# Moving the second gram and the row of norms by one tile in a fused graph attention with a residual layer norm

## What is computed

```python
z_l = x @ W_lang.T ;  z_g = x @ W_grav.T ;  v = x @ W_V.T            # per batch of x
zn  = z_l / max(norm(z_l), EPS)
A_l = max(zn @ zn.T, 0) * not_eye
d2  = max(sq + sq.T - 2 * z_g @ z_g.T, 0)                            # sq = row sums of z_g * z_g
A_g = exp(-d2 / (2 * sigma**2)) * not_eye
K   = w_l * row_stochastic(A_l * adj) + (1 - w_l) * row_stochastic(A_g * adj)
out = layernorm(x + (K @ v) @ W_O.T)                                 # over the last axis
```

## Time and profile before

| | us |
|---|---|
| median of 3 runs | 969.12 (967.76 to 969.14) |
| the profiled execution | 971.3 |
| span of the profile | 969.6 |
| busy: TensorE / VectorE / ScalarE / GpSimd | 956.4 / 699.6 / 323.6 / 146.3 |

### The profile page before, as it was taken

The page is one execution under the profiler, slowest core; times in us unless marked ns, Lnnn a source line. Parts: engine busy times, 40 slices in busy tenths (PEclk is TensorE's granted clock), DMA queues, the critical chain, the costliest instruction groups (busy, mean ns, idle before and its releaser), DMA issues.

```text
span 969.6 us, 13226 instructions
## 1 busy us (share of the span) xinstructions
PE 956.4 (99%) x4802; PEld 827.4 (85%) x4802; DVE 699.6 (72%) x1954; ACT 323.6 (33%) x632; POOL 146.3 (15%) x155
## 2 busy tenths in 40 slices
PE   9999999999999999999999999999999999999997
PEld 7888888988888888888888889888888988889885
DVE  4567768767785777858677786777858767685588
ACT  5333243232422423243232432423233232432331
POOL 2002120021200212110021200212101121200231
PEclk9999999999999999999999999999999999999999
DMA  8322353442534434353442534434344442533001
GB/s 218 86 61 80 100 144 101 114 154 86 120 109 114 147 101 119 108 141 99 120 143 81 136 105 119 146 98 122 107 114 126 120 131 93 136 98 120 1 23 66
DMA packets 215872, 106.78 MB, mean 110 GB/s; under 512 B 140544, under 2 KB 187648, under 8 KB 215808
## 3 DMA queue, kind: packets, MB, share of 16 engines
q1 hardware_dynamic: 189504, 92.04, 34.1%
q10 hardware_dynamic: 26304, 13.90, 4.9%
HBM read 63.44 MB, written 42.47 MB: 109 GB/s over the span
## 4 chain that ended last, share of the span: by engine, by line
PE 90%; DVE 5%; DMA 3%; issue 1%; ACT 0%; POOL 0%; ACTq 0%; POOLq 0%; SPq 0%; DVEq 0%
PE ring L333 22%; PE ring L334 22%; PE ring L335 22%; PE g_bank L333 8%; PE g_bank L335 8%; PE g_bank L334 8%; DMA off<-off_turned 1%; DMA off_turned<-off 1%; DMA k_turned<-ag 1%; PE g_bank L328 1%; DVE al L928 1%; DVE al L905 0%; DVE bn L966 0%; DVE kT_lo L761 0%; DMA y<-in_x_dram 0%
## 5 line engine op out<-in xcount | busy, mean ns | idle before, releaser
L747 DVE TENSOR_TENSOR zg_lo<-ring,zg_hi 128x512 fp32r<-128x512 f32 x64 | 43.9, 690 | 103.3 <-ACT zg_hi L575 103.2
L1180 POOL TENSOR_TENSOR rstd<-var_eps,neg_half 128x1 f32<-128x1 f32 x64 | 41.5, 650 | 416.7 <-DVE var_eps L974 416.7
L333 PE MATMUL ring<-xT_hi,wgT_hi 128*128 128x512 f32 x256 | 102.0, 398 | 0.0
L333 PE MATMUL ring<-xT_hi,wlT_hi 128*128 128x512 f32 x256 | 101.1, 395 | 0.0
L334 PE MATMUL ring<-xT_lo,wgT_hi 128*128 128x512 f32 x256 | 100.1, 391 | 0.0
L335 PE MATMUL ring<-xT_hi,wgT_lo 128*128 128x512 f32 x256 | 99.8, 390 | 0.0
L334 PE MATMUL ring<-xT_lo,wlT_hi 128*128 128x512 f32 x256 | 99.7, 390 | 0.0
L335 PE MATMUL ring<-xT_hi,wlT_lo 128*128 128x512 f32 x256 | 99.7, 390 | 0.0
L333 PE MATMUL ring<-wvo_hi,xT_hi 128*128 128x512 f32 x256 | 99.7, 389 | 0.0
L335 PE MATMUL ring<-wvo_hi,xT_lo 128*128 128x512 f32 x256 | 99.6, 389 | 0.0
L334 PE MATMUL ring<-wvo_lo,xT_hi 128*128 128x512 f32 x256 | 99.6, 389 | 0.0
(11 more groups left out here) (126 smaller groups left out, 2211.9 us busy)
## 6 DMA issues: line engine op xcount, KB each, us to landing
xb<-in_x_dram SPq DMA_DIRECT2D x60, 256.0 KB, 4.6
out_dram<-y SPq DMA_DIRECT2D x60, 256.0 KB, 2.0
k_turned<-ag SPq DMA_DIRECT2D x56, 256.0 KB, 2.5
y<-in_x_dram SPq DMA_DIRECT2D x14, 1024.0 KB, 7.1
off_turned<-off SPq DMA_DIRECT2D x28, 384.0 KB, 2.3
al<-k_turned SPq DMA_DIRECT2D x112, 64.0 KB, 2.3
al<-k_turned ACTq DMA_DIRECT2D x112, 64.0 KB, 2.6
off<-off_turned SPq DMA_DIRECT2D x56, 96.0 KB, 2.4
```

Of the source, the lines that this page charges most:

```text
L333: nc.tensor.matmul(psum, lh, rh, start=k == 0, stop=False)
L747: nc.vector.tensor_tensor(pair[1][:, i, :], bank[:, :], pair[0][:, i, :].bitcast(F32), ALU.subtract).then_inc(evacuated, 1)
L1180: nc.gpsimd.tensor_tensor(rstd[:, i:i + 1], var_eps[:, i:i + 1], neg_half[:, 0:1], ALU.pow)\
```

## The change

In each of the batches 0 to 13 TensorE's `gram_l` moves behind zg tile 3 (it was ahead of it), and the row of norms moves behind zl tile 0 (it was ahead of it). The ring order `BATCH` swaps these two tiles; `LAST`, which had them so already, keeps its order. ScalarE reads zg tile 3 out ahead of `widen_r` instead of behind it, zl tile 0 ahead of the fetch of the off blocks, and zl tile 1 ahead of the mirror copies. VectorE's splits move likewise: zg tile 3 ahead of the diagonals, zl tiles 0 and 1 ahead of `mask_al`; the four steps of `mask_ag` are mixed with the diagonals in another way. SyncE's and GpSimd's orders stay as they are; no instruction is added or removed.

```diff
--- before.py
+++ after.py
@@ -60,11 +60,11 @@
 
 
 
-BATCH = ([("zg", 1, 0), ("hsq", 0, 0), ("zg", 1, 1), ("zg", 1, 2), ("zg", 1, 3), ("r", 0, 0), ("zl", 1, 0),
+BATCH = ([("zg", 1, 0), ("hsq", 0, 0), ("zg", 1, 1), ("zg", 1, 2), ("zg", 1, 3), ("zl", 1, 0), ("r", 0, 0),
           ("zl", 1, 1), ("zl", 1, 2), ("zl", 1, 3), ("u", 1, 0), ("u", 1, 1), ("u", 1, 2), ("u", 1, 3)]
          + [("out", 0, i) for i in range(4)])
 
-LAST = (BATCH[:5] + [BATCH[6], BATCH[5]] + BATCH[7:10]
+LAST = (BATCH[:10]
         + [("u", 1, 0), ("kT", 0, 0), ("kT", 0, 1), ("out", 0, 0), ("hsq", 1, 0), ("kT", 0, 2), ("kT", 0, 3),
            ("out", 0, 1), ("out", 0, 2), ("r", 1, 0), ("u", 1, 1), ("u", 1, 2), ("u", 1, 3), ("kT", 1, 0),
            ("out", 0, 3), ("kT", 1, 1), ("out", 1, 0), ("kT", 1, 2), ("out", 1, 1), ("kT", 1, 3), ("out", 1, 2),
@@ -504,10 +504,11 @@
                 s.hsq_as_rows(0)
                 s.project("zg", 1)
                 s.project("zg", 2)
+                s.project("zg", 3)
                 s.gram_l(0)
-                s.project("zg", 3)
+                s.project("zl", 0)
                 s.r_as_rows(0)
-                for i in range(T):
+                for i in range(1, T):
                     s.project("zl", i)
                 for i in range(T):
                     s.project("u", i)
@@ -674,14 +675,15 @@
                 s.exp(0, 1)
                 s.exp(0, 2)
                 s.exp(0, 3)
+                s.hi("zg", 1, 3, zg)
                 s.widen_r(0)
                 s.scale_ag(0, range(1))
-                s.hi("zg", 1, 3, zg)
+                s.hi("zl", 1, 0, zl)
                 fetch_off(act, "l", s.b, ACT_PARTS)
                 s.scale_ag(0, range(1, T))
-                s.hi("zl", 1, 0, zl)
+                s.hi("zl", 1, 1, zl)
                 s.copy_mirrors("l", gl_copied, range(T))
-                for i in range(1, T):
+                for i in range(2, T):
                     s.hi("zl", 1, i, zl)
                 s.hi("u", 1, 0, u[1 - parity])
                 fetch_k(act, b, 0, ACT_PARTS)
@@ -989,21 +991,21 @@
                     s.exponent(0, i, copied=True)
                 s.mask_ag(0, 0)
                 s.lo("zg", 1, 2, zg)
+                s.mask_ag(0, 1)
+                s.lo("zg", 1, 3, zg)
+                s.mask_ag(0, 2)
                 s.diagonals(0, gl_rows, 1.0, nsq, gl_diag, [0], turned=gl_off)
-                s.mask_ag(0, 1)
-                s.mask_ag(0, 2)
+                s.mask_ag(0, 3)
                 s.diagonals(0, gl_rows, 1.0, nsq, gl_diag, [1], turned=gl_off)
-                s.mask_ag(0, 3)
+                s.scale_of_ag(0)
                 s.diagonals(0, gl_rows, 1.0, nsq, gl_diag, [2], turned=gl_off)
-                s.scale_of_ag(0)
                 s.diagonals(0, gl_rows, 1.0, nsq, gl_diag, [3], turned=gl_off)
                 s.clamp_norms(0)
-                s.lo("zg", 1, 3, zg)
+                s.lo("zl", 1, 0, zl)
                 s.repeat_row("r", 0)
-                s.lo("zl", 1, 0, zl)
+                s.lo("zl", 1, 1, zl)
                 s.mask_al(0, 0, copied=True)
                 s.mask_al(0, 1)
-                s.lo("zl", 1, 1, zl)
                 s.mask_al(0, 2)
                 s.mask_al(0, 3)
                 s.scale_of_al(0)
```

## The result

| | before | after |
|---|---|---|
| median of 11 runs, us | 967.83 (967.37 to 969.60) | 976.54 (972.24 to 977.98) |
| profiled execution, us | 971.3 | 977.83 |
| span of the profile, us | 969.6 | 976.1 |

The ratio of the changed kernel to the one before is 1.0076, 95% interval 1.0062 to 1.0091: slower by 0.76%, some 7.4 us; the two medians of the table lie 8.7 us apart. 975.7 was forecast, from 970.0 to 980.5.

The account below looks back on a forecast made before the run. The prediction took TensorE, busy 956.4 of 969.6 us, to bound the kernel. Its terms, -4.16 + 7.7 + 3.1 = +6.6 us, added to a median of 969.12, gave 975.7 us, range 970.0 to 980.5.

Parts of the forecast that it names:

- The gain: Second gram's waits for VectorE's exponent in batches 4, 7 and 11 all go: -4.16 us.
- The margin: Exponent's spare time before the second gram, to grow from 0.6 to 3.3 us.
- The row of norms, cost 0: On TensorE, r_wide and the r transpose move alike, one tile still between gram and r transpose: cost 0.
- The shift of 2.66 us, fixed by GpSimd's fourth tile: Fourth mask_al on VectorE starts 2.66 us later, held by GpSimd's fourth mask_r tile until 849.76 in batch 13.
- It goes through whole to kT tile 0: From the fourth mask_al through turn_k, k store, ScalarE's fetch and kT_hi to kT_lo, the 2.66 us passes undiminished.
- First aggregate tile, 7.7 us: TensorE waits for kT tile 0 before the first aggregate tile: 0.24 us in batch 13, 7.7 us over 14 batches.
- Second aggregate tile, 3.1 us: TensorE waits for kT tile 1 before the second aggregate tile: 0.37 us in batch 13, 3.1 us over 14 batches.
- VectorE late into the next batch, cost 0: VectorE enters the next batch some 1.7 us late, putting 0.4 us on the off transfer, within 3.3 us: cost 0.
- The sum: Whole kernel: -4.16 + 7.7 + 3.1 = +6.6 us, giving 975.7 us.
- The clock: Rival: after long waits in batches 3 and 10, aggregate tiles run at 1.2 GHz: +5.4, 981 us, chance 0.03.
- the signs of being wrong: First kT_lo under 2.4 us later, VectorE idle before mask_al not for GpSimd, TensorE waits elsewhere, granted clock below 1.00.
- The faster rival: mask_r's fourth tile does not hold mask_al, or k stores land sooner: shift 1.66, -2.1 us, 967.0 us, chance 0.09.

Follow-up runs that it names:

- its control: Kernel before, with mask_r's tile 0 made by VectorE instead of GpSimd: 968.43 us, ratio 0.9994.
- VectorE's tile: Kernel after, with mask_r's tile 0 made by VectorE, so that GpSimd makes three tiles: 967.28 us, ratio 0.9982 to the kernel before.
- four extra tiles: Kernel before, with four extra GpSimd tiles of mask x row ahead of its four, in batches 0 to 13: 1016.74 us, a single run.

## Why the prediction was right, point by point

- **The gain.** Right in the profile: the second gram waited in none of 14 batches, 4.16 us by the view of waits, 5.0 us by batch lengths. The margin held a slow transfer too: in batches 4, 7 and 11 the first exponent began at 15.85, 15.14 and 15.88 in the batch, over a microsecond late, and the gram still began at 18.10. In timed runs the gain is smaller: with the late path shortened in both orders it measured 1.9 us.
- **The row of norms, cost 0.** Right: r came one tile behind the gram's end as before, and nothing waited for it.
- **The shift of 2.66 us, fixed by GpSimd's fourth tile.** Right to 0.01 us at the combine. That GpSimd and not VectorE holds it was argued; the run with three tiles on GpSimd shows it (0.74 us earlier and all the loss gone), the run with VectorE's order put back shows the other half.
- **It goes through whole to kT tile 0.** Right: 2.63 us in batch 13 (43.93 to 46.56). From the end of kT_lo to the first matmul it takes 0.15 us (867.66 to 867.81), where the prediction took 0.04 from a wait of the gram; over 14 batches that is 1.5 us which its sum lacks. That ScalarE's queue is part of the path is shown by the run that turned it over.
- **First aggregate tile, 7.7 us.** 7.3 us by the starts of the first aggregate tile; the clean batches waited 0.27 to 0.36 us where 0.14 to 0.63 was forecast. The sizes by batch were off: forecast were 1.7 us in batches 3 and 10 and 0.8 in 7; measured were 2.6 in batch 10, 0.9 in batch 1, and no more than in a clean batch in 3 and 7. So part of the agreement is luck: what 3 and 7 did not cost pays for the 0.15 us above and for batch 1. Batch 1 has another cause than a slow store: its off blocks landed at 33.05 in the batch, 1.5 us later than in most. They did so (32.83 to 33.15) in all six traces with the gram behind zg tile 3, and in none of the six with the old order (28.7 to 29.0, as in most batches there). What they meet there is not known.
- **Slow transfers come in the same batches.** In each of the 12 traces the first trip of the off blocks landed late in batches 4 and 7 (14.06 to 16.72 in the batch, where 13.2 to 13.9 is usual), and in 8 of them one of the first three stores of k in batch 10 took 3.2 to 4.5 us. So batch 10 could be foreseen from the trace of before, and its size could not; batch 3 was slow in the trace of before and in its control, and in none with the gram moved.
- **Second aggregate tile, 3.1 us.** The term mis-sized. By the start of kT_lo 1 plus 0.68 and 0.15 us, the second tile waited for kT tile 1 in four batches only (0, 2, 3 and 4), 0.65 us in all; in batch 13 kT tile 1 was ready 0.43 us ahead. Its shift was taken as 2.66 but was 2.08 in batch 13 (47.03 to 49.11): the last store of k, issued 3.0 us later (41.29 to 44.31), was followed by ScalarE's fetch only 2.0 us later (44.89 to 46.87), so it landed sooner after its issue. What came in the term's place was not in the sum: a tile that begins behind a wait takes 0.1 us longer, at the first aggregate tile in every batch and at the second in four, some 1.8 us. With the 0.65 that makes the 2.5 us that are left of the excess of 11.2 behind the first tile's waits (7.3) and the clock (1.4).
- **VectorE late into the next batch, cost 0.** Right: its first store of off blocks was issued at 7.81 to 8.01 in the batch, against 7.81 to 7.87.
- **The sum.** 10.8 us of waits forecast, 11.2 measured, but the measured one has 3.2 us that were not in the sum, 1.4 of slow clock in batch 10 and 1.8 of restarts, and the forecast one 2.4 us at the second tile that did not come. That the two agree to 0.4 us is luck; that clean batches would pay some 0.4 us each and no more is not (58.35 to 58.43 for 58.4). The level agrees in part by luck too: the median of before that it started from, 969.12 of 3 runs, was 967.83 in 11.
- **The clock, and the signs of being wrong.** A granted clock below 1.00 was named as such a sign, and it came: 0.56 behind the wait of batch 10. The price of one fall, 2.7 us, had been taken too high, since about seven of twelve matmuls ran slow. As a rival it had a chance of 0.03; it came once in this trace. The row that was to speak against it, 1.00 around a wait of 1.61 us, said nothing of waits of 2.4. The granted clock of the runs fits this: five runs between 972.2 and 974.5 us had 0.998 to 1.000, the six from 976.5 to 978.0 had 0.996 to 0.998. How much of the gap between the two groups is the clock's stays open, since a slow store, which brings the long wait, costs by itself.
- **The faster rival.** It said that below a shift of 2.1 the change pays. VectorE's tile brought the shift to 1.9, and the kernel became faster than before. That fits the break-even point but does not place it: no run lies between 1.9 and 2.66, and the gain it was reckoned with, 4.16 us, was 1.9 in timed runs.

## What to carry to other kernels

Moving work behind a late operand gives cover at one wait and takes it at another: before doing it, follow what hangs on the moved work to its next fixed deadline and compare the room there with the shift, with the slowest gate on the way, which may be an engine that is 15% busy. Lateness below the room cost nothing here (1.3 and 1.9 us) and above it cost in every batch, so a gain in 3 of 14 batches can be paid for in all 14. Once the gate is shortened, the same move pays; an in-order queue with waits for later data in front of ready work is a cheap place to find that room.

## What was not expected of the hardware

- A wait of TensorE of 2.49 us in front of the aggregate was followed by seven matmuls at about 1.2 GHz (1.4 us lost), one of 2.36 us with four extra tiles by some eight (4.43 us for a tile), and one of 2.51 us with VectorE's order put back by none. The timeline of that third run, at the same place in batch 10:

```profile
690.05 0.47 PE L333 MATMUL ring<-u_even_hi,kT_hi 128*128 128x512 f32 x1 [2.51 <-DVE kT_lo L943]
690.36 0.40 PE L334 MATMUL ring<-u_even_lo,kT_hi 128*128 128x512 f32 x1
690.59 0.39 PE L335 MATMUL ring<-u_even_hi,kT_lo 128*128 128x512 f32 x1
```

  The matmuls follow at 0.23 us. The granted clock stood at 1.00 there (690.0 to 693.4). So the clock fell behind waits of 2.36 and 2.49 us and not behind one of 2.51; behind waits of 1.47 to 1.60 us, in the other 13 batches of the run with four extra tiles, no aggregate tile was slow.
- GpSimd's multiplication of 128 x 512 goes from 1296 to between 1730 and 1797 ns when VectorE's, of 692 ns with two SBUF operands, runs beside it.
- Behind a wait of TensorE the first two matmuls of a 128 x 512 tile begin 0.31 us apart instead of 0.23, at full clock.
